# Own orders of steps for the last group of a four-layer cross-attention kernel

## The reference

```python
# layer 0: over channels, 64x64 weights, one head, inputs normalised along 256
A = softmax(einsum('bct,bcs->bts', conv(Wn, inorm(x)), conv(Wm, inorm(ctx))))
x = conv(Wo, einsum('bcs,bts->bct', conv(Wl, ctx), A)) + x
# layers 1 and 2: 16 heads of 16 features, keys and values from layer_norm(ctx)
Q = x @ Wq.T;  K = layer_norm(ctx) @ Wk.T;  V = layer_norm(ctx) @ Wv.T
x = x + tanh(gate) * (softmax(Q K^T * 16**-0.5, masked) V) @ Wo.T
# layer 3: one head of 256 features
x = x + alpha * (softmax((x w_q^T)(ctx w_k^T)^T / 16) (ctx w_v^T)) @ w_o^T
```

## Time and profile before

| | |
|---|---|
| three runs | 605.64, 607.59, 608.26 us; median 607.59 |
| the profiled execution | 605.95 us, its span 604.1 us |
| mean granted TensorE clock | 0.987 of full speed |
| TensorE busy (matmul) | 563.6 us, 93% of the span |
| VectorE, ScalarE, GpSimd busy | 470.9 (78%), 462.9 (77%), 115.1 us (19%) |

### The profile page before, as it was taken

The page is one execution under the profiler, slowest core; times in us unless marked ns, Lnnn a source line. Parts: engine busy times, 40 slices in busy tenths (PEclk is TensorE's granted clock), DMA queues, the critical chain, the costliest instruction groups (busy, mean ns, idle before and its releaser), DMA issues.

```text
span 604.1 us, 26503 instructions
## 1 busy us (share of the span) xinstructions
PE 563.6 (93%) x11087; PEld 498.1 (82%) x11087; DVE 470.9 (78%) x1063; ACT 462.9 (77%) x961; POOL 115.1 (19%) x130
## 2 busy tenths in 40 slices
PE   3598999999999999999999999999999999999975
PEld 2387888988888888988889888988889888888864
DVE  3497869878797869878797869879797869877654
ACT  0784879968798778968798778968798778878662
POOL 5401061101601061100601052100701052000000
PEclk9998999999999999999999999999999999999979
DMA  8220000210020100210020100210010100010001
GB/s 241 80 77 1 3 3 2 78 38 3 2 77 2 38 2 2 77 37 3 2 70 9 38 1 3 77 38 2 2 54 25 38 1 3 3 38 1 3 2 36
DMA packets 18501, 18.35 MB, mean 30 GB/s; under 512 B 1828, under 2 KB 18340, under 8 KB 18404
## 3 DMA queue, kind: packets, MB, share of 16 engines
q1 hardware_dynamic: 17216, 16.26, 8.5%
q0 software_dynamic: 320, 0.26, 0.3%
q10 hardware_dynamic: 868, 0.30, 0.2%
HBM read 12.63 MB, written 4.19 MB: 28 GB/s over the span
## 4 chain that ended last, share of the span: by engine, by line
PE 75%; ACT 12%; DVE 5%; issue 3%; ACTq 2%; DMA 1%; DVEq 0%
PE psum L385 13%; PE psum L675 11%; PE psum L729 10%; PE psum L387 10%; PE psum L386 10%; ACT work L856 5%; PE psum L722 4%; PE psum L642 4%; PE psum L655 3%; ACT v L805 3%; PE psum L465 2%; PE psum L450 2%; PE psum L522 1%; ACTq L927 1%; DVE shifted L1037 1%
## 5 line engine op out<-in xcount | busy, mean ns | idle before, releaser
L1033 DVE TENSOR_REDUCE negmax<-psum 128x8 f32<-128x512 f32 x128 | 87.2, 681 | 11.5 <-PE psum L655 11.5
L1037 DVE TENSOR_TENSOR shifted<-psum,negmax 128x512 f32<-128x512 f32 x128 | 88.5, 691 | 5.3
L870 ACT ACTIVATE work<-psum,group_mask 128x512 f32<-128x512 f32 x128 | 80.3, 698 | 10.0 <-PE psum L675 9.6
L856 ACT ACTIVATE work<-shifted 128x512 f32<-128x512 f32 x128 | 75.3, 631 | 3.2 <-DVE shifted L1037 2.1
L675 PE MATMUL psum<-const,work 64*128 64x64 f32 x1536 | 65.2, 228 | 12.6 <-ACT work L856 9.0
L675 PEld LDWEIGHTS psum<-const,work 64*128 64x128 f32 x1536 | 56.3, 141 | 24.6 <-ACT work L856 14.6
L729 PEld LDWEIGHTS psum<-v,work 128*64 128x64 f32 x2048 | 63.0, 138 | 7.6 <-issue 3.0
L729 PE MATMUL psum<-v,work 128*64 128x34 f32 x2048 | 67.6, 225 | 0.8 <-ACT work L870 0.8
L805 ACT ACTIVATE v<-psum 64x256 f32<-64x256 f32 x128 | 49.7, 388 | 20.3 <-PE psum L387 19.1
L851 ACT ACTIVATE work<-psum,negmax 128x256 f32<-128x256 f32 x128 | 50.7, 482 | 5.6 <-DVE negmax L1029 5.3
L797 ACT ACTIVATE kbd<-psum,own_bias,const 128x512 f32<-128x512 f32 x64 | 46.6, 791 | 0.3 <-PE psum L387 0.3
(11 more groups left out here) (179 smaller groups left out, 1517.4 us busy)
## 6 DMA issues: line engine op xcount, KB each, us to landing
x_raw<-in_x_dram SPq DMA_DIRECT2D x8, 512.0 KB, 4.3
c_raw<-in_ctx_dram SPq DMA_DIRECT2D x8, 512.0 KB, 5.4
out_dram<-attn SPq DMA_DIRECT2D x16, 256.0 KB, 2.2
mrow_u<-in_mask_dram SPq DMA_DIRECT2D x8, 64.0 KB, 5.0
kbd<-in_L_xattn_Wq_dram SPq DMA_DIRECT2D x2, 256.0 KB, 9.5
kbd<-in_L_xattn_Wk_dram SPq DMA_DIRECT2D x2, 256.0 KB, 9.9
kbd<-in_L_xattn_Wv_dram SPq DMA_DIRECT2D x2, 256.0 KB, 11.1
kbd<-in_L_xattn_Wo_dram SPq DMA_DIRECT2D x2, 256.0 KB, 11.2
```

Source lines behind the costliest of these rows:

```text
L856: act.activation(probs[:, exp_row(g, l, i, last), :], shifted[:, i % 4, :], ACT.Exp).then_inc(exps, 1)
L870: act.activation(probsT[:, at, :], o[:], ACT.Copy, scale=group_mask[:, 2 * i + c:2 * i + c + 1]).then_inc(free, 1)
L1033: dve.tensor_reduce(negmax[:, i % 2, :], sv, AX_X, ALU.max, negate=True).then_inc(rowmax, 1)
L1037: dve.tensor_tensor(shifted[:, i % 4, :].rearrange("t (j k) -> t j k", k=C), sv, negmax[:, i % 2, :].unsqueeze(2).broadcast_to([P, NJ, C]) ...
```

## The change

The last group gets tables of its own (`PE_TAIL`, `ACT_TAIL`, `DVE_TAIL`) with the same steps as before, in another order; `steps` loses its second argument. Tables of the repeated part and the prologue stay.

```diff
-AHEAD = ("H", 0), ("H", 1), ("L", 0), ("L", 1), ("Q1", 0)
-NEXT = ("xT", "cT", "nT", "Mn", "Mm", "V0", "K1", "ST", "MV")
-
-
-def steps(table, front):
+PE_TAIL = """
+    V2.0 S1.0-3 V1.0 Q1.1 V3.0 S1.4-7 T1.0-1 A1.0 V1.1 A1.1 T1.2-3 AT1.0 K2.0 O1.0 A1.2-3 K2.1 AT1.1 Q2.0 O1.1 S2.0-3 V2.1
+    K3.0 Q2.1 S2.4-7 T2.0-1 K3.1 A2.0-1 T2.2-3 AT2.0 A2.2-3 O2.0 AT2.1 V3.1 O2.1 S3.0-1 XN.0-1 T3.0-1 PV.0-1
+"""
+ACT_TAIL = """
+    V2.0 X1.0 V1.0 Q1.1 X1.1-3 V3.0 SC.0 T1.0 X1.4 T1.1 X1.5-7 V1.1 AT1.0 T1.2-3 H.2 K2.0 AT1.1 K2.1 Q2.0 H.3 V2.1 X2.0-1
+    Q2.1 X2.2 K3.0 X2.3 T2.0-1 X2.4-7 K3.1 T2.2-3 AT2.0-1 V3.1 X3.0-1 T3.0-1 XN.0-1
+"""
+DVE_TAIL = """
+    S1.0-7 A1.0-1 AT1.0 O1.0 A1.2-3 L.2 AT1.1 O1.1 S2.0 L.3 S2.1-7 A2.0-1 AT2.0 A2.2-3 O2.0 AT2.1 O2.1 S3.0-1 X3.0-1
+    PV.0-1
+"""
+
+
+def steps(table):
...
-        if not front and (name in NEXT or attends and name[1:] == "0"):
-            continue
         for i in range(int(first), int(last) + 1):
-            if not front and (name, i) in AHEAD:
-                continue
...
-    PE_STEPS, PE_LAST = steps(PE_ORDER, True), steps(PE_ORDER, False)
-    ACT_STEPS, ACT_LAST = steps(ACT_ORDER, True), steps(ACT_ORDER, False)
-    DVE_STEPS, DVE_LAST = steps(DVE_ORDER, True), steps(DVE_ORDER, False)
-    PE_PROLOGUE, ACT_PROLOGUE, DVE_PROLOGUE = steps(PE_FIRST, True), steps(ACT_FIRST, True), steps(DVE_FIRST, True)
+    PE_STEPS, PE_LAST = steps(PE_ORDER), steps(PE_TAIL)
+    ACT_STEPS, ACT_LAST = steps(ACT_ORDER), steps(ACT_TAIL)
+    DVE_STEPS, DVE_LAST = steps(DVE_ORDER), steps(DVE_TAIL)
+    PE_PROLOGUE, ACT_PROLOGUE, DVE_PROLOGUE = steps(PE_FIRST), steps(ACT_FIRST), steps(DVE_FIRST)
```

## The result

| | before | after |
|---|---|---|
| runs (median of 4 each) | 606.62 us (605.01 to 608.26) | 599.82 us (599.51 to 600.14) |
| ratio, 95% interval | | 0.987 (0.984 to 0.990) |
| the profiled execution | 605.95 us, span 604.1 | 600.14 us, span 598.3 |
| start of the last group (its first V matmul) | 539.98 us | 539.92 us |
| last group, from there to the end of the span | 64.1 us | 58.4 us |

The kernel became faster by 1.3%. Between the two profiled executions it is 5.8 us, all of it in the last group (64.1 - 58.4 = 5.7). Lines of the code have moved by 6 (L655 is L661 now, L1033 is L1039; by 3 or 4 in those experiments that use the old lists).

A forecast was written before the change was run, and what follows sets the result against it. TensorE, busy 93% of the span, was taken as the bound, with waits in the last group removable: 4.85 + 0.5 - 0.1 = 5.3 us off the 606.8 us median gives 601.5 us, range 599 to 605.

The forecast's parts named there:

- S2.0-3 earlier, K3.0 gone: TensorE, last group: with K3.0 out of the middle, S2.0-3 come 0.75 us earlier, bounds 0 to 0.94.
- end of S2.3, with S2.0 ahead of L.3: VectorE: S2.3 ends at 573.74 instead of 574.96, 1.2 us earlier, for this order and K3.0's move together.
- VectorE's wait for S2.4: VectorE, second scores: with S2.4-7 ahead of T2.0 on TensorE, it waits 0.15 us instead of 3.78.
- end of S2.7: VectorE: S2.7 ends at 579.55 instead of 584.40, 4.85 us earlier, the 1.2 us at S2.3 included.
- AT2.0 ahead of A2.2: ScalarE no longer waits 0.45 us for AT2.0, so its copies and O2.0 come earlier: 0.5 us gained.
- V3.1 ahead of O2.1: TensorE: V3.1, about 1.5 us, goes into the 1.38 us wait ahead of O2.1: -0.1 us.
- V2.0 before V1.0: zero: TensorE, first half: swapping these 12-matmul steps, with X1.0 between them on ScalarE, changes nothing: zero.
- the paragraph on the clock: TensorE, last group: half clock follows the 3.01 us wait, not waits of 0.85 to 1.38; new order costed at 2.4 GHz.
- rival 3: Slower: TensorE stays at 1.2 GHz from Q2.1 to the end, costing 9.2 us, so 610.7 us; chance 0.04.
- Rivals 1: ScalarE becomes the bound in the second scores, up to 2 us at X2.7: gain 3.3, 603.5 us; chance 0.13.
- Rival 2: S2.4-7 waits behind Q2.1's copy, so VectorE's wait moves instead of going: gain 2.7, 604.1 us; chance 0.12.
- Rival 4: Order does nothing: another bank or buffer holds S2.4-7 until X2.3, 606.8 us; chance 0.03.

The follow-up runs named there:

- the main edit: Old order of all engines with only S2.4-7 put ahead of T2.0 on TensorE: last group 60.5 us, 3.6 less than before; ratio 0.9925.
- V3.1 early: Changed kernel with V3.1 back behind Q2.1 on TensorE and behind X2.3 on ScalarE: last group 59.6 us, 1.2 more.

## Why the prediction was right or wrong

The direction was right, and so was the chain of waits with the place of every step. The size was too small, for the profiled execution by a little and for the runs by more: a gain of 5.3 us was forecast, with bounds of 2.7 to 6.3; the profiled pair shows 5.8, the medians 6.8 and the ratios 7.7 to 7.9. What the clock does in the old kernel was wrong.

Step by step in the profile (each difference to a time before less the 0.06 us by which the last group starts earlier; the first three rows are parts of the fourth, and the last three make the sum):

| step | forecast | measured |
|---|---|---|
| S2.0-3 earlier, K3.0 gone | 0.75 | 567.02 - 566.02 - 0.06 = 0.94 |
| end of S2.3, with S2.0 ahead of L.3 | 1.2 | 574.96 - 573.43 - 0.06 = 1.47 |
| VectorE's wait for S2.4 | 0.15 | 573.49 - 573.43 = 0.06 |
| end of S2.7 | 4.85 | 584.40 - 579.15 - 0.06 = 5.2 |
| AT2.0 ahead of A2.2 | 0.5 | (590.08 - 584.27) - (585.12 - 579.86) = 0.55 |
| V3.1 ahead of O2.1 | -0.1 | (593.52 - 587.78) - (590.08 - 584.27) = -0.07 |
| sum | 5.3 | 5.7 |

The term mis-sized here is the 0.75: I took off 0.2 for Q2.0's copy, which did not end last, and that 0.2 runs on to the end of S2.3 and of S2.7. By their own experiments K3.0 alone is worth 1.6 us, L.3 0.4, AT2.0 0.5 and the main edit 3.6 us, each in other surroundings, so they need not add up to 5.7. "V2.0 before V1.0: zero" and the order of A1.0 and V1.1 stand for 0.5 us together, through a bank that I had not followed. That the sum held here all the same is luck: it began from the changed order, in which that bank is free.

The step that failed is the paragraph on the clock, and with it the base of the sum. I took one profiled execution for the old kernel: one fall, 575 to 581, and full speed "behind the waits of 0.85 to 1.38 us". I wrote that this execution was one of the quick ones, and then took its gain of 5.3 us off the median of all four, as if a slower execution had no more to lose. In the third profile of the same kernel the clock fell behind 0.85 us as well, with 66.2 us for the last group; over four profiles it takes 63.1, 64.1, 64.1 and 66.2, on average 64.4, against 58.4 and 58.4. That makes 6.0 us of the 7.7 to 7.9 that the ratios give. Four profiles are few, and they were quick ones: they took 606.6 us on average, the 56 other runs of the old kernel on record 607.8 (604.2 to 612.4), and the ten of the changed kernel 599.9 (598.6 to 601.3). So about 1.2 us of the runs' gain lies in executions that no profile shows, and some 0.7 in the start of the last group, 540.4 on average in the old kernel's four profiles and 539.7 in the changed one's two, on the same code. That it is further falls of the clock in the last group of the slowest ones, of 609 to 612 us, is argued and not shown, since none was profiled beyond 609.06. I had priced such falls only for the changed kernel, as rival 3, and not as something that the old kernel pays in many executions and the change takes away. Against all this the forecast of 601.5 us was 1.7 us high (599.82).

The Trainium skill, TensorE: Matmul & The Clock Gate, section "A second HAM failure mode", says that short idle times between groups, while banks are cycled, can make the clock swing. The runs here agree with it for the old order (a fall behind 0.85 us in two kernels) and for the first half (behind 0.84 us in one execution each of two kernels, 0.66 and 0.69 granted in the stretch from 550 to 555); in the changed order's second half no profile shows a fall. I had set it aside by one trace.

Rivals 1 and 2 did not come: X2.7 starts 0.03 us after S2.7, VectorE waits 0.06 us. Rival 2's mechanism is real, though: in "V3.1 early" one fill more moved the wait instead of removing it. Rival 3 did not come in the changed kernel's profiles, and a first-half fall as in two of its variants cost 1.5 us, not 9.2. Rival 4 did not come either.

## What to carry to other kernels

The last pass of a pipelined loop deserves an order of its own: steps that were placed as cover for a next group's work become head-of-line waits once that work is gone; here one such turn ahead of the scores cost 3.6 us. In a chain of short steps with a rotation of buffers, moving one step changes who waits for which buffer some steps later, so follow the buffers as well as the orders. And where TensorE is often idle, take more than one profile of the old kernel before sizing a gain: what the clock takes differs from one execution to the next.

## What the runs showed that was not expected

Filling TensorE's longest wait with useful and repeated matmuls did not help: the clock then fell further on, at T2.2 or A2.2, and cost more there (3.4 and 2.6 us, against 1.3 at T2.0), so that the last group took 66.2 and 66.5 us instead of 64.1, the latter with 1.1 us that the filling itself cost. The fall has no fixed place: behind a wait of 3.0 us it came at once in two profiles of the old kernel, after T2.0 in the other two, and behind waits of 0.84 to 0.85 us it came in some executions and not in others.
